# TensorE turns the identity matrix at the entry of the attention and of the closing stage of a five-stage layer pair

## The reference

```
x = x + 0.5 * L0_ffn(layernorm(x))     # 64 experts, top 8, 128 slots each
x = x +       L0_attn(layernorm(x))    # 16 heads, 64 memory slots
x = x + 0.5 * L0_ffn(layernorm(x))     # the same experts again
x = x + 0.5 * L1_ffn(layernorm(x))     # gated, inner width 688, weights looked up in a table of 16
x = x +       L1_attn(layernorm(x))    # gated linear recurrence
x = x + 0.5 * L1_ffn(layernorm(x))
```

## Time and profile before

| what | value |
|---|---|
| three runs | 2724.72, 2729.47, 2734.68 us (median 2729.47) |
| the profiled execution's own time | 2733.78 us |
| its span, first to last instruction | 2731.9 us |
| mean granted clock of TensorE | 0.944 |
| busy: PE, PEld, DVE, ACT, POOL | 87%, 77%, 66%, 32%, 46% |

### The profile page before, as it was taken

The page is one execution under the profiler, slowest core; times in us unless marked ns, Lnnn a source line. Parts: engine busy times, 40 slices in busy tenths (PEclk is TensorE's granted clock), DMA queues, the critical chain, the costliest instruction groups (busy, mean ns, idle before and its releaser), DMA issues. The chain is left out here.

```text
span 2731.9 us, 44553 instructions
## 1 busy us (share of the span) xinstructions
PE 2390.3 (87%) x16926; PEld 2116.9 (77%) x16926; DVE 1798.4 (66%) x3578; ACT 865.1 (32%) x1704; POOL 1244.1 (46%) x1214
## 2 busy tenths in 40 slices
PE   6565579999999999999999999986566488999997
PEld 6444469999999999999999999976455377888886
DVE  5433358888888888888888888865422256676654
ACT  4322223333333333333333333323322132333332
POOL 3277735554555455545554555452278612222110
PEclk9988789999999999999999999995599889999999
DMA  6799710000000000000000000004599700000000
GB/s 205 236 240 228 173 26 5 17 21 20 5 17 20 21 5 17 21 20 5 16 21 17 9 17 20 13 3 134 156 242 217 153 26 24 24 24 24 16 9 16
DMA packets 196930, 169.52 MB, mean 62 GB/s; under 512 B 28944, under 2 KB 189680, under 8 KB 196208
## 3 DMA queue, kind: packets, MB, share of 16 engines
q1 hardware_dynamic: 167040, 118.69, 14.8%
q0 software_dynamic: 24576, 37.77, 7.5%
q10 hardware_dynamic: 5104, 10.22, 1.2%
HBM read 117.94 MB, written 53.13 MB: 63 GB/s over the span
## 5 line engine op out<-in xcount | busy, mean ns | idle before, releaser
L968 POOL TENSOR_TENSOR a_orstd<-a_ms,minus_half 128x8 f32<-128x8 f32 x64 | 106.8, 1669 | 492.6 <-DVE a_ms L1128 492.5
L948 POOL TENSOR_SCALAR a_pick<-a_index,lut_row 128x258 f32<-128x258 int32 x240 | 281.4, 1172 | 24.3
L1121 DVE RECIPROCAL a_rz<-a_rz 128x256 f32<-128x256 f32 x128 | 215.6, 1716 | 0.0
L776 DVE TENSOR_TENSOR e_hT<-e_psH,e_sil 128x128 f32<-128x128 f32 x128 | 37.3, 291 | 264.8 <-ACT e_sil L733 174.1
L652 PE MATMUL e_psX<-ident,e_xg 128*128 128x128 f32 x256 | 62.8, 333 | 169.1 <-DMA e_xg<-rows,slot_tok 167.6
L652 PEld LDWEIGHTS e_psX<-ident,e_xg 128*128 128x128 f32 x256 | 31.3, 159 | 217.3 <-DMA e_xg<-rows,slot_tok 212.4
L1330 PEld LDWEIGHTS a_psD<-a_v,a_at 128*128 128x128 f32 x1536 | 181.3, 192 | 7.2 <-issue 1.5
L951 POOL TENSOR_TENSOR a_found<-a_found,a_pick 128x258 f32<-128x258 f32 x240 | 177.5, 740 | 20.0
L1330 PE MATMUL a_psD<-a_v,a_at 128*128 128x128 f32 x1536 | 181.8, 275 | 1.2 <-DVE a_at L1101 1.2
L622 POOL DMA_INDIRECT e_xg<-rows,slot_tok x128 | 128.8, 1006 | 109.4 <-POOLq L247 66.1
L1101 DVE TENSOR_TENSOR a_at<-a_psB,causal 128x384 f32<-128x384 f32 x256 | 130.2, 550 | 48.8 <-PE a_psB L1267 48.8
(11 more groups left out here) (261 smaller groups left out, 7730.4 us busy)
## 6 DMA issues: line engine op xcount, KB each, us to landing
e_wg<-in_L_ffn_w_gate SPq DMA_DIRECT2D x128, 128.0 KB
e_wu<-in_L_ffn_w_up SPq DMA_DIRECT2D x128, 128.0 KB
e_wd<-in_L_ffn_w_down SPq DMA_DIRECT2D x128, 128.0 KB
rows<-r_row SPq DMA_DIRECT2D x32, 320.0 KB, 3.2
stream_b<-r_zeros SPq DMA_DIRECT2D x11, 384.0 KB, 5.7
stream_c<-rows SPq DMA_DIRECT2D x33, 128.0 KB, 3.2
r_xt<-in_L_attn_hidden_states SPq DMA_DIRECT2D x16, 256.0 KB, 3.6
stream_a<-r_xt SPq DMA_DIRECT2D x16, 256.0 KB, 4.5
```

The source lines that it names most:

```text
L948: nc.gpsimd.tensor_scalar(pick[:, :, :], index[:, :, :], float(c), w["lut"][:, c:c + 1], ALU.is_equal, ALU.mult).then_inc(picked, 1)
L968: nc.gpsimd.tensor_tensor(out=flat(orstd[:, :, :]), in0=ms[:, :], in1=cst["minus_half"][:, 0:TT * HQ], op=ALU.pow).then_inc(orstd_ok, 1)
L1121: nc.vector.reciprocal(rz[:, a, :], rz[:, a, :]).then_inc(rz_ok, 1)
```

## The change

TensorE gets a helper in both blocks that turns the identity matrix n times. In the attention it runs 50 times ahead of `turn_stream(0)` and 10 times behind it, into the first 128 columns of psD. In the closing it runs 70 times ahead of `turn(IN, 0, 0)` and 20 times behind it, into the first 128 columns of psY[0]. The helper waits for nothing and signals nothing. No other engine's list changes.

```
@@ attention, block.tensor
+                def occupy(n):
+
+                    for k in range(n):
+                        nc.tensor.transpose(psD[:, 0, 0:P], ident, ident)
+
+                occupy(50)
                 turn_stream(0)
+                occupy(10)
                 value(0, 0)
                 slots(0)
@@ closing, block.tensor
+                def occupy(n):
+
+                    for k in range(n):
+                        nc.tensor.transpose(psY[0][:, 0:P], cst["ident"][:, :], cst["ident"][:, :])
+
+                occupy(70)
                 turn(IN, 0, 0)
+                occupy(20)
                 for i in range(U + 2):
```

## The result

The changed kernel takes 2725.64 us (median of 20 runs, 2719.54 to 2731.88), the kernel before 2731.22 in the 20 runs beside it (2724.72 to 2737.88). The ratio is 0.9979, 95% interval 0.9971 to 0.9987: faster by 5.6 us, 3.5 to 7.9. The forecast was 6.35 us, to 2723.1 from the 2729.47 that was then the median of three runs. A second measurement later gave 0.9977 (0.9966 to 0.9989), 6.3 us.

The account below looks back on a forecast made before the run. TensorE, busy for 87% of the span, was taken to bound the kernel; 0.52 + 2.12 + 0.93 + 2.78 = 6.35 us off the 2729.47 median gives 2723.1 us, 0.23% faster, range 2718 to 2738.

Parts of the forecast that it names:

- Whether turns raise the clock: At both entries: turns alone raise TensorE's clock from half to full speed, with lags of 4.4 or 5.9 us assumed.
- The rival of a clock that stays low: Both entries: turns, like the routers' busy half-speed mix, never raise the clock; 7.0 us lost, 2736.5 us; chance 0.22.
- Free of cost under the wait: Both entries: the 50 and 70 turns end before the awaited rows, within 9.4 and 11.4 us of room, costing nothing.
- The turns of rows: At full speed, four in the attention take 0.60 for 1.12 us, eight in the closing 1.04 for 1.97.
- The closing's products: Closing's first 15 matmuls of 512 columns take 3.47 us at full speed in place of 6.25, gaining 2.78.
- the gain is kept to the end: Later units are bound by TensorE and start relative to the entries, so the whole 6.35 us reaches the kernel's end.
- The attention's products: Attention's 24 matmuls ahead of query take 4.19 us at full speed in place of 6.31, gaining 2.12.
- the idle time that is left is 0.8 to 1.8 us, so I take it that the clock stays up: Both entries: the idle time between the added turns ahead and the rows is too short to drop the clock.
- half of it: The clock drops again or rises late at one entry; only 2.64 or 3.71 us gained, about 2726; chance 0.14.
- The second fill: The 10 and 20 turns fit with 0.5 and 0.1 us, keeping activity up over gaps of 1.4 or 2.2 us.
- What a measurement can tell: Whole kernel: about 0.3% (8.2 us) can be told from no change; forecast and all rivals lie inside it.

## Why the prediction was right, and where not

*Whether turns raise the clock,* the point on which all hung: they do. At both entries of every trace with the fills it rose, 2.7 to 5.9 us after the first turn, with nothing but turns on TensorE. The rival of a clock that stays low is refuted; its argument from the routers fits the 64-column matmuls, which left the clock low here too. With it falls, for these float32 turns, the rule of the Trainium skill, "TensorE: Matmul & The Clock Gate", Part 4, that the full clock does not engage for transposes.

*Free of cost under the wait:* right. The fifty and seventy were over before the rows in every trace, 0.7 to 2.8 us before where nothing stood between; the row turns began 9.35 and 11.44 us after their block's first load, 9.42 and 11.42 before.

*The turns of rows,* 0.52 and 0.93 us: measured 0.46 and 0.88 (0.66 for four, 1.09 for eight; the first of a row took a little longer than in the merged rows that I priced them by).

*The closing's products,* 2.78: with the turns 3.71 were forecast. The 16th product came 18.2 us after SP's first load, 21.8 before: 3.6 us. The first store shows 2.6 of it in the first trace and 3.1 in the second, 2.7 in both if taken from the start of the row turns. One more drop of the clock, from 2202.4 to 2205.8 just behind `gate_up`, lies in between; the trace of before has none there (1.00 from 2203 to 2210). So "the gain is kept to the end" failed for 0.9 us of it.

```profile
2202.00:2206.00 4.00, 3.55 (x17) 3.55 (x18) 2.46 (x6) 0.34 (x1) 0.00 (x0) 0.57 0.01 2
```

*The attention's products,* 2.12, is the step that failed. It rested on "the idle time that is left is 0.8 to 1.8 us, so I take it that the clock stays up". I had the lag from two rises behind dense products, 4.4 and 5.9 us. It was 3.3 here (3.7 in the second trace), and a quicker rise makes the fifty shorter (7.23 us), so the gap came to 2.06 us and the clock fell 0.8 us behind it. Query came 1.5 us sooner after the first load (16.77 for 18.26), not 2.64: the rival "half of it", in part. In the second trace the gap was 1.90 us and the clock fell likewise. Where the clock held, query came 6.4 us behind the start of the row turns for 8.8 before, 2.4 us of the 2.64 forecast: the size of the term was right, and the clock that it assumed was not. The Trainium skill, "TensorE: Matmul & The Clock Gate", "Why this matters for your kernels", asks for no idle gaps above some 3 us. That would have passed this gap of 2.06 us; the trace disagrees, and the measurement decides.

*The second fill.* I counted it as something that fits and may not be needed. The two comparisons without it say that without it nothing measurable is left of the gain, though the traces explain only a part of that.

*What a measurement can tell.* I put that at 8.2 us; with twenty runs on either side the interval was 2.2 us either way, so a gain well below 8.2 was told from none.

In sum, 6.35 us were forecast, 5.6 and 6.3 measured. That nearness is in part luck. The two traces of the changed kernel show 1.3 us at the attention's third load and 2.7 at the closing's first store, 4.0 together. Where the rest comes from is not shown: other runs may have kept the clock where these two lost it, and drops elsewhere move too, as in the attention's last unit, which took 167.5 us from its last load to its last store in both of them and 169.1 in the trace of before.

## What to carry to other kernels

TensorE's wait for a stage's first data can be used to bring its clock up, at no cost as long as the filling ends before the data is there, also for the slowest rise; what is gained is half the time that its first products now take, and only where they are the chain. Size the fill for the slow case. A fill of fixed count ends soonest when the clock rises soonest, and leaves the longest gap: the fifty that took 7.0 to 7.4 us were followed by gaps of 1.9 to 2.7 us and a fall, those that took 7.5 to 8.5 by gaps of 0.7 to 1.5 and none. Tying a last part to a semaphore shortly ahead of the data closes that gap in the traces; what it saves in time was too small to be told here. Fill the wait behind the turns too, and with work that raises the clock, not with 64-column matmuls.

## What the runs showed of the hardware

Turns of 128 float32 columns raised the clock 2.7 to 5.9 us after the first, at both entries of all traces that had them; 64-column float32 matmuls at the same pace (0.21 us a record, no gap) did not in 10.9 us. Once it was up, the clock outlasted the gaps ahead of the row turns of up to 1.5 us, and one of 1.75 in the closing; around gaps of 1.90, 2.06 and 2.73 us in the attention and 2.81 in the closing it fell, in three of the four only 0.8 to 1.2 us into the work behind the gap; with the 2.17 us ahead of the closing's first product left empty it fell as well, both times. The step of a turn was 0.11 and 0.21 us at the two levels. And of two executions of one kernel, one can drop the clock at an entry where the other does not (without the second fill, the attention: a rise after 5.9 us and no fall, a rise after 2.8 us and a fall), so that one trace tells what can happen and not what the median holds.
